# Two grouped-norm convolutions on one core: 32-wide products of both convolutions side by side, roots ahead of mid's normalization, x bands normalized on ScalarE

## The chip, the core and the metric

The kernel runs on one core of a Trainium2 chip. The metric is the device time of one launch in microseconds (us). Before the change the median of three runs is 901.29 us (901.25 to 901.67). Engines are called as the profile calls them: PE is TensorE (matmuls), PEld its weight loads, DVE is VectorE, ACT is ScalarE, POOL is GpSimd, SP is the engine that here only issues DMAs. Two independent runs of one kernel agree within about 0.2%.

## The reference

```python
def _gn(v, G=16, eps=1e-05):            # 32 channels, groups of 2
    g = v.reshape(B_, G, C_ // G, H_, W_)
    m = jnp.mean(g, axis=(2, 3, 4), keepdims=True)
    s = jnp.var(g, axis=(2, 3, 4), keepdims=True)
    return ((g - m) / jnp.sqrt(s + eps)).reshape(v.shape)
x = x + _L0_conv_ref(_gn(x), L0_conv_weight, L0_conv_threshold)   # 3x3, weights masked by a threshold
x = x + _L1_conv_ref(_gn(x), L1_conv_kernel, L1_conv_bias)        # 5x5, written with FFTs, plus bias
```

x is (16, 32, 128, 128) in float32. Both convolutions keep 32 channels and pad with zeros. The 5x5 one is written as a product of Fourier transforms, but is a plain 5x5 convolution of the padded image. The value between the two blocks is called mid.

## The kernel before

**Tiling.** An image is cut into two halves of 64 rows, so there are 32 halves (`HALVES`), half h being half h % 2 of image h // 2. A half lies in SBUF as four bands of 16 rows, one on each quarter of the 128 partitions (32 channels each), with 1 row of halo on each side for the 3x3 (`x_bands`, 6 slots, 128x2304 elements) and 2 rows for the 5x5 (`mid_bands`, 3 slots, 128x2560).

**Products in float16.** A float32 band is split into a float16 high part (`x3_hi`, `x5_hi`, written by ACT in `high3`, `high5`) and a float16 remainder (`x3_lo`, `x5_lo`, written by DVE in `low3`, `low5`); the weights likewise (`s3_hi`, `s3_lo`, `s5_hi`, `s5_lo`). Three products are summed in PSUM: high x high, high image x low weights, low image x high weights. There is one buffer of each of these four images, so the next one may be written only when PE has read the last one. The 3x3 sums lie in PSUM banks 0 to 3, the 5x5 sums in banks 4 to 7.

**pairs and singles.** A weight tile is 32 input channels (a quarter of the rows of the array) by either 64 columns (`pairs`, line 773: two neighbouring kernel rows at once, for two quarters of the output rows) or 32 columns (`singles`, line 791: the kernel row that is left over). Every matmul streams 512 columns. For one product of a half, the 3x3 takes 48 matmuls of each sort, the 5x5 160 pairs and 80 singles.

**The steps.** At step s PE does the 3x3 of half s and the 5x5 of half s - 3 (`LAG` = 3). Steps 0 to 2 are the lead (`lead_high`, `lead_low` and the small blocks between them, with only the 3x3), steps 3 to 31 run a loop body, `whole_step`, and steps 32 to 34 a second body, `last_steps`, with only the 5x5. Inside `whole_step` the order is high image 3x3, high image 5x5, low image 3x3, low image 5x5. A 3x3 result is taken out of PSUM by DVE (`take_conv3`, line 651, which adds x and makes mid); its drain (line 654) raises `bank3_go`, without which PE may not start the next step. A 5x5 result is taken by ACT (`take_conv5`, line 424) after `b5_whole`, POOL adds it to mid (line 360), SP stores it.

**Statistics.** DVE takes bn_stats of x (`stats_in`, line 560) and of mid (`stats_out`, line 659). Once per two steps the per-partition moments go through DRAM (`spread_stats`, `gather_stats`, issued by ACT) and come back to all partitions (`every_mv`). DVE then forms the group variance (`group_stats`, lines 592 to 600), ACT takes its square root (`take_root`, line 372) and DVE makes scale and bias from it (`scale_of`, lines 607 to 614). This is done in even steps s (where `exchanged(s - 1)` is not empty), for mid of the image just finished and for x of a coming image. `normalize3` scales a slot of x_bands in place (DVE, line 621), `normalize5` a slot of mid_bands (ACT, line 394).

**What sets the order.** Each engine runs its own program in the order in which it is written, and waits on semaphores; there is no planner. ACT's and DVE's order inside a step is that of the loops at lines 446 to 483 and 730 to 757. SP issues, in each step: the store of half s - 4, the load of x bands of half s + 6 (line 251, which waits on `norm1`), the moves of mid into mid_bands (16 DMAs from SBUF to SBUF, line 259), and x for half s + 2.

## Time and profile before

| | |
|---|---|
| median of three runs | 901.29 us |
| the profiled execution | 901.0 us |
| its span, first to last instruction | 899.2 us |
| mean granted clock of PE | 0.955 of full speed |
| PE busy / PEld busy | 794.9 us (88%) / 508.1 us (57%) |
| DVE busy | 611.0 us (68%) |
| ACT busy | 336.1 us (37%) |
| POOL busy | 234.5 us (26%) |
| bytes moved by DMA | 150.59 MB, mean 167 GB/s |
| chain that ended last | PE 75%, DVE 8%, issue 7%, ACT 4% |

Matmuls overlap one another in the array, so that the busy time of one (about 381 ns) says nothing of its cost; the distance from the start of one group of matmuls to the start of the next does. The chain that ended last follows the work back from the last instruction; a share of DVE and ACT in it is time in which PE was waiting for them.

### The profile page before, as it was taken

Reading aid. Unit: us, or ns where it says so; the run is one execution under the profiler, and the core shown is the slowest. Engines: PE = TensorE matmul, PEld = TensorE weight load, DVE = VectorE, ACT = ScalarE, POOL = GpSimd, SP = SyncE. Lnnn points to the kernel's source line nnn. Section 1 sums busy time; section 2 is a strip of 40 time slices with the busy share of each in tenths; the row PEclk is TensorE's granted clock in tenths of the full one; section 3 lists DMA queues with packets and bytes.
Section 4 is the critical chain, followed back from the end, with each engine's and each line's share of the span. In section 5 each row is a group of like instructions: output and inputs, shape, how many; then the busy total and the mean of one; then the engine's idle time right before and its main releaser. Section 6 shows DMA issues by size and latency. Waiting matters only on the chain.

```text
span 899.2 us, 67768 instructions
## 1 busy us (share of the span) xinstructions
PE 794.9 (88%) x32302; PEld 508.1 (57%) x32302; DVE 611.0 (68%) x949; ACT 336.1 (37%) x289; POOL 234.5 (26%) x165
## 2 busy tenths in 40 slices
PE   0785698989899898989899898989899898997895
PEld 0342365656567565756566575656566565664463
DVE  6676398786767697676767687686767585664141
ACT  0342234353524244353524244353524244352320
POOL 1014042322303232321303232321303232333031
PEclk9887999999999999999999999999999999999898
DMA  8989875978788686878888676978886554664313
GB/s 182 207 178 227 172 154 141 210 171 204 182 191 209 156 181 161 192 181 194 189 196 197 148 186 163 210 181 192 191 197 163 131 134 113 148 156 97 72 47 93
DMA packets 234118, 150.59 MB, mean 167 GB/s; under 512 B 18592, under 2 KB 227552, under 8 KB 229984
## 3 DMA queue, kind: packets, MB, share of 16 engines
q1 hardware_dynamic: 228768, 144.67, 70.3%
q10 hardware_dynamic: 4608, 4.23, 1.9%
q0 software_dynamic: 704, 1.25, 0.6%
q8 instruction: 16, 0.26, 0.1%
q14 instruction: 22, 0.18, 0.1%
HBM read 75.60 MB, written 33.59 MB: 121 GB/s over the span
## 4 chain that ended last, share of the span: by engine, by line
PE 75%; DVE 8%; issue 7%; ACT 4%; DVEq 2%; DMA 1%; POOL 1%; SPq 1%; ACTq 0%; POOLq 0%
PE psum L773 56%; PE psum L791 19%; ACT x_hi L379 3%; DVE mid L651 2%; DVEq L654 2%; DMA x_bands<-x_dram 1%; DVE bn_out L659 1%; DVE bn_in L560 1%; DVE x_lo L631 1%; ACT root L372 0%; SPq L251 0%; DVE x_lo L639 0%; DVE rinv L607 0%; DVE newton L609 0%; DVE newton L608 0%
## 5 line engine op out<-in xcount | busy, mean ns | idle before, releaser
L360 POOL TENSOR_TENSOR mid<-mid,conv_out 128x512 f32<-128x512 f32 x122 | 216.8, 1806 | 598.4 <-ACT conv_out L424 598.4
L773 PE MATMUL psum<-x_hi,s_hi 32*64 32x512 f16 x6656 | 211.8, 399 | 47.6 <-DVEq L654 37.8
L773 PE MATMUL psum<-x_hi,s_lo 32*64 32x512 f16 x6656 | 206.9, 391 | 1.9 <-issue 1.9
L773 PE MATMUL psum<-x_lo,s_hi 32*64 32x512 f16 x6656 | 200.7, 381 | 2.6 <-issue 2.6
L773 PEld LDWEIGHTS psum<-x_hi,s_hi 32*64 32x64 f16 x6656 | 107.1, 107 | 137.9 <-DVEq L654 44.6
L773 PEld LDWEIGHTS psum<-x_hi,s_lo 32*64 32x64 f16 x6656 | 126.9, 109 | 72.6 <-issue 16.0
L379 ACT ACTIVATE x_hi<-x_bands 128x2304 f16<-128x2304 f32 x32 | 68.0, 2126 | 265.4 <-PE psum L791 262.4
L651 DVE SCALAR_TENSOR_TENSOR mid<-psum,unscale,x_own 128x1024 f32<-128x1024 f32 x64 | 79.2, 1279 | 127.0 <-PE psum L791 126.5
L773 PEld LDWEIGHTS psum<-x_lo,s_hi 32*64 32x64 f16 x6656 | 111.7, 104 | 76.0 <-issue 13.9
L424 ACT ACTIVATE conv_out<-psum,bias,unscale 128x512 f32<-128x512 f32 x122 | 85.1, 777 | 61.4 <-PE psum L773 38.5
L639 DVE TENSOR_TENSOR x_lo<-mid_bands,x_hi 128x2560 f16<-128x2560 f32 x32 | 99.0, 3094 | 0.8 <-PE psum L773 0.5
L631 DVE TENSOR_TENSOR x_lo<-x_bands,x_hi 128x2304 f16<-128x2304 f32 x32 | 97.9, 3061 | 0.0
L791 PE MATMUL psum<-x_hi,s_hi 32*32 32x512 f16 x4096 | 76.1, 382 | 15.5 <-issue 9.0
L394 ACT ACTIVATE mid_bands<-mid_bands,nbias,gscale 128x2560 f32<-128x2560 f32 x32 | 80.8, 2524 | 22.1 <-DVE nbias L614 19.5
L387 ACT ACTIVATE x_hi<-mid_bands 128x2560 f16<-128x2560 f32 x32 | 74.8, 2339 | 36.8 <-PE psum L791 32.1
L659 DVE BATCH_NORM_STATS2 bn_out<-mid 128x6 f32<-128x512 f32 x128 | 79.1, 681 | 4.1
L791 PE MATMUL psum<-x_hi,s_lo 32*32 32x512 f16 x4096 | 78.1, 387 | 2.5 <-issue 2.5
L560 DVE BATCH_NORM_STATS2 bn_in<-x_bands 128x6 f32<-128x512 f32 x128 | 77.9, 668 | 1.3 <-DMA x_bands<-x_dram 1.1
L791 PEld LDWEIGHTS psum<-x_hi,s_hi 32*32 32x32 f16 x4096 | 52.5, 88 | 37.5 <-issue 24.8
L791 PE MATMUL psum<-x_lo,s_hi 32*32 32x512 f16 x4096 | 67.2, 381 | 2.0 <-issue 2.0
L791 PEld LDWEIGHTS psum<-x_hi,s_lo 32*32 32x32 f16 x4096 | 61.8, 88 | 5.2 <-issue 3.4
L791 PEld LDWEIGHTS psum<-x_lo,s_hi 32*32 32x32 f16 x4096 | 49.9, 88 | 23.3 <-issue 18.0
(77 smaller groups left out, 267.9 us busy)
## 6 DMA issues: line engine op xcount, KB each, us to landing
x_own<-x_dram SPq DMA_DIRECT2D x128, 256.0 KB, 5.0
mid_bands<-mid SPq DMA_DIRECT2D x372, 80.0 KB, 2.1
out_dram<-mid SPq DMA_DIRECT2D x116, 256.0 KB, 5.5
x_bands<-x_dram SPq DMA_DIRECT2D x96, 288.0 KB, 6.1
x_bands<-x_dram SPq DMA_DIRECT2D x32, 272.0 KB, 6.4
mid_bands<-mid SPq DMA_DIRECT2D x124, 64.0 KB, 2.0
every_mv<-mv_scratch ACTq DMA_DIRECT2D x16, 256.0 KB, 3.7
out_dram<-mid SPq DMA_DIRECT2D x24, 128.0 KB, 2.4
```

Of the source, the lines that this page charges most:

```text
L360: nc.gpsimd.tensor_tensor(m, m, conv_out[:, b, :], ALU.add).then_inc(out_added, 1)
L379: nc.scalar.activation(x3_hi[:, :, 2:2 + W], x_bands[:, h % XB_SLOTS, :, :], ACT.Copy).then_inc(hi3_done, 1)
L387: nc.scalar.activation(x5_hi[:, :, 2:2 + W], mid_bands[:, k % MB_SLOTS, :, :], ACT.Copy).then_inc(hi5_done, 1)
L394: nc.scalar.activation(v, v, ACT.Identity, bias=nbias[:, at], scale=gscale[:, at]).then_inc(act_scaled, 1)
L424: nc.scalar.activation(conv_out[:, b, :], psum[:, X5_BANK + b, :], ACT.Identity, bias=bias[:, 0:1], scale=unscale[:, 1:2]).then_inc(conv5_ ...
L560: nc.vector.bn_stats(bn_in[:, h // 2 % 2, h % 2, b, :], rows.rearrange("p a w -> p (a w)")).then_inc(bn_x, 1)
L631: nc.vector.tensor_tensor(x3_lo[:, :, 2:2 + W], x_bands[:, h % XB_SLOTS, :, :], x3_hi[:, :, 2:2 + W], ALU.subtract).then_inc(x3_lo_go, 1)
L639: nc.vector.tensor_tensor(x5_lo[:, :, 2:2 + W], mid_bands[:, k % MB_SLOTS, :, :], x5_hi[:, :, 2:2 + W], ALU.subtract).then_inc(x5_lo_go, 1)
L651: nc.vector.scalar_tensor_tensor(mid[:, h % MID_SLOTS, at, :], psum[:, X3_BANK + at.start:X3_BANK + at.stop, :], unscale[:, 0:1], x_own[:, ...
L659: nc.vector.bn_stats(bn_out[:, h % 2, b, :], mid[:, h % MID_SLOTS, b, :]).then_inc(bn_mid, 1)
L773: ins = nc.tensor.matmul(psum[2 * C * J:2 * C * (J + 1), bank + i, :].rearrange("p (a w) -> p a w", a=A), w[quad(i), at:at + 2, :].rearran ...
L791: ins = nc.tensor.matmul(psum[quad(j), bank + i, :].rearrange("p (a w) -> p a w", a=A), w[quad(i), at, :], src[quad(i), j + dy:j + dy + A ...
```

## The change

1. **PE.** Inside `whole_step` the order becomes: all pairs of the 3x3 (high and low image), the high-image pairs of the 5x5, all singles of the 3x3, all singles of the 5x5, and the low-image pairs of the 5x5. `last_steps` and the lead are ordered likewise. A new semaphore, `high3_whole`, tells when PE has read x3_hi for the last time; x5_hi is free after the 5x5's singles.
2. **ACT.** x bands are normalized on ACT (`normalize3` in the loop), after the 5x5 result is taken. Both square roots of an even step come before mid's normalization.
3. **DVE.** `normalize3` is left only for half 0. In an even step DVE forms both group variances, then both scales. `stats_in` of two halves is done in odd steps. `low3(s + 1)` stands at the end of step s and no longer in step s + 1. Its semaphore is split in two: one for SP (which frees the slot of x_bands) and one for PE behind a drain.
4. **Lead.** The scale of the 5x5 weights is formed before the second `take_conv3`, and PE's first block (`lead_start`) is placed in the program behind the lead's other blocks.

What PE's loop body is, before and after (x_hi with s_hi or s_lo is a high-image product, x_lo a low-image one; 64x512 is a pair, 32x512 a single). Before:

```order
L773 MATMUL psum<-x_hi,s_hi 64x512 x48
L773 MATMUL psum<-x_hi,s_lo 64x512 x48
L791 MATMUL psum<-x_hi,s_hi 32x512 x48
L791 MATMUL psum<-x_hi,s_lo 32x512 x48
L791 MATMUL psum<-x_hi,s_hi 32x512 x80
L791 MATMUL psum<-x_hi,s_lo 32x512 x80
L773 MATMUL psum<-x_hi,s_hi 64x512 x160
L773 MATMUL psum<-x_hi,s_lo 64x512 x160
L773 MATMUL psum<-x_lo,s_hi 64x512 x48
L791 MATMUL psum<-x_lo,s_hi 32x512 x128
L824 REGISTER_ALU
L773 MATMUL psum<-x_lo,s_hi 64x512 x160
```

After, the same body on the same engine:

```order
L777 MATMUL psum<-x_hi,s_hi 64x512 x48
L777 MATMUL psum<-x_hi,s_lo 64x512 x48
L777 MATMUL psum<-x_lo,s_hi 64x512 x48
L777 MATMUL psum<-x_hi,s_hi 64x512 x160
L777 MATMUL psum<-x_hi,s_lo 64x512 x160
L795 MATMUL psum<-x_hi,s_hi 32x512 x48
L795 MATMUL psum<-x_hi,s_lo 32x512 x48
L795 MATMUL psum<-x_lo,s_hi 32x512 x128
L795 MATMUL psum<-x_hi,s_hi 32x512 x80
L795 MATMUL psum<-x_hi,s_lo 32x512 x80
L834 REGISTER_ALU
L777 MATMUL psum<-x_lo,s_hi 64x512 x160
```

The counts are the same; the body goes from 64 to 32 columns or back four times before and twice after, the last block joining the next step's first.

What ACT does in an even step, from taking the 5x5 result on (line 372 is a root, line 394 a normalization, 379 and 387 the high parts of x and mid). Before:

```order
L424 ACTIVATE conv_out<-psum,bias,unscale 128x512 x4
L437 DMA every_mv<-mv_scratch 128x512
L372 ACTIVATE root<-gvar 128x1
L394 ACTIVATE mid_bands<-mid_bands,nbias,gscale 128x2560
L416 ACTIVATE mid_bands<-zeros 32x256
L379 ACTIVATE x_hi<-x_bands 128x18x128
L387 ACTIVATE x_hi<-mid_bands 128x20x128
L372 ACTIVATE root<-gvar 128x1
```

After, the same step:

```order
L424 ACTIVATE conv_out<-psum,bias,unscale 128x512 x4
L437 DMA every_mv<-mv_scratch 128x512
L394 ACTIVATE x_bands<-x_bands,nbias,gscale 128x2304
L404 ACTIVATE x_bands<-zeros 32x128
L372 ACTIVATE root<-gvar 128x1 x2
L394 ACTIVATE mid_bands<-mid_bands,nbias,gscale 128x2560
L416 ACTIVATE mid_bands<-zeros 32x256
L379 ACTIVATE x_hi<-x_bands 128x18x128
L387 ACTIVATE x_hi<-mid_bands 128x20x128
```

The second root has moved from behind both high parts to in front of mid's normalization, and the normalization of x bands is new on this engine.

What DVE does from the last variance of an even step to the start of the next step. Before:

```order
L600 SCALAR_TENSOR_TENSOR gvar<-sums 128x1
L560 BN_STATS bn_in<-x_bands 128x6 x4
L607 RECIPROCAL rinv<-root 128x1
L608 TENSOR_TENSOR newton<-gvar,rinv 128x1
L609 TENSOR_TENSOR newton<-newton,rinv 128x1
L610 TENSOR_SCALAR newton<-newton 128x1
L611 SCALAR_TENSOR_TENSOR gscale<-rinv,newton 128x1
L651 SCALAR_TENSOR_TENSOR mid<-psum,unscale,x_own 128x1024 x2
L659 BN_STATS bn_out<-mid 128x6 x4
L639 TENSOR_TENSOR x_lo<-mid_bands,x_hi 128x20x128
L631 TENSOR_TENSOR x_lo<-x_bands,x_hi 128x18x128
```

After, from the second scale of the same step on:

```order
L611 RECIPROCAL rinv<-root 128x1
L612 TENSOR_TENSOR newton<-gvar,rinv 128x1
L613 TENSOR_TENSOR newton<-newton,rinv 128x1
L614 TENSOR_SCALAR newton<-newton 128x1
L615 SCALAR_TENSOR_TENSOR gscale<-rinv,newton 128x1
L617 SCALAR_TENSOR_TENSOR nbias<-gmean,gscale 128x1
L656 SCALAR_TENSOR_TENSOR mid<-psum,unscale,x_own 128x1024 x2
L664 BN_STATS bn_out<-mid 128x6 x4
L635 TENSOR_TENSOR x_lo<-x_bands,x_hi 128x18x128
L644 TENSOR_TENSOR x_lo<-mid_bands,x_hi 128x20x128
```

The 3x3's low part (`x_lo<-x_bands`) now stands in front of the 5x5's, which begins the next step.

The diff, cut to its core:

```diff
@@ SP, in step s
                 if has3(s + XB_SLOTS):
-                    sp.wait_ge(norm1, s + 2)
+                    sp.wait_ge(low3_done, s + 1)
                     load_bands(s + XB_SLOTS)
@@ ACT: high3, high5
                 if h:
-                    act.wait_ge(c3_whole, h)
+                    act.wait_ge(high3_whole, h)
...
                 if k:
-                    act.wait_ge(b5_begun, k)
+                    act.wait_ge(a5_whole, k)
@@ ACT, in step s
+                if s == LAG:
                     take_root(gathered[0])
+                if s >= LAG and has3(s + 1):
+                    normalize3(s + 1)
+                if gathered and s > LAG:
+                    for stat in gathered:
+                        take_root(stat)
...
-                if len(gathered) > 1:
-                    take_root(gathered[1])
@@ DVE: low3
                 nc.vector.tensor_tensor(x3_lo[:, :, 2:2 + W], x_bands[:, h % XB_SLOTS, :, :], x3_hi[:, :, 2:2 + W],
-                                        ALU.subtract).then_inc(x3_lo_go, 1)
+                                        ALU.subtract).then_inc(low3_done, 1)
+                dve.drain().then_inc(x3_lo_go, 1)
@@ DVE, the lead
+            dve.wait_ge(w_loaded, 16 * 2 * Q)
+            largest(w5, 1)
+            power_of_two(1)
+            nc.vector.drain().then_inc(w5_bounded, 1)
             take_conv3(1)
-            stats_out(0)
             low3(2)
+            stats_out(0)
             stats_out(1)
             aggregate("mid", 0, mean_go)
-            dve.wait_ge(w_loaded, 16 * 2 * Q)
-            largest(w5, 1)
-            power_of_two(1)
-            nc.vector.drain().then_inc(w5_bounded, 1)
+            take_conv3(2)
             mean_of(("mid", 0))
-            take_conv3(2)
@@ DVE, in step s
                 low5(s - LAG)
-                if has3(s):
-                    low3(s)
                 if gathered:
                     dve.wait_ge(mv_in, 16 * exchange_number(s - 1))
-                    group_stats(gathered[0])
-                    scale_of(gathered[0])
-                if has3(s + 1):
-                    normalize3(s + 1)
+                for stat in gathered:
+                    group_stats(stat)
                 if len(gathered) > 1:
-                    group_stats(gathered[1])
-                if has3(s + 5):
-                    stats_in(s + 5, range(BANKS))
-                if len(gathered) > 1:
-                    scale_of(gathered[1])
+                    dve.wait_ge(norm1, s + 2)
+                for stat in gathered:
+                    scale_of(stat)
+                if s % 2:
+                    for h in (s + 3, s + 4):
+                        if has3(h):
+                            stats_in(h, range(BANKS))
                 if has3(s):
                     take_conv3(s)
                     stats_out(s)
...
+                if has3(s + 1):
+                    low3(s + 1)
@@ PE
+            def singles3():
+
+                singles(s3_hi, x3_hi, K3, X3_BANK)
+                singles(s3_lo, x3_hi, K3, X3_BANK).then_inc(high3_whole, 1)
                 singles(s3_hi, x3_lo, K3, X3_BANK).then_inc(c3_whole, 1)
...
+            def singles5():
 
                 pe.wait_ge(x5_lo_go, 1)
-                singles(s5_hi, x5_lo, K5, X5_BANK).then_inc(b5_begun, 1)
+                singles(s5_hi, x5_lo, K5, X5_BANK)
+                singles(s5_hi, x5_hi, K5, X5_BANK)
+                singles(s5_lo, x5_hi, K5, X5_BANK).then_inc(a5_whole, 1)
...
             with nc.body("whole_step", valid_engines=only):
                 hint = pe.mark_branch_hint_location()
-                high_image3()
-                high_image5()
-                low_image3()
-                low_image5(step)
+                pairs3_high()
+                pairs3_low()
+                pairs5_high()
+                singles3()
+                singles5()
+                pairs5_low(step)
```

## Rows read from the trace of the kernel before

**Rows 1.** Waits, longest first in total (us in total, times, longest).
```profile
DVE rinv L607 <- ACT root L372: 58.1, 32, 6.4
PE psum L773 <- DVEq L654: 37.8, 14, 2.8
```

**Rows 2.** Timeline (start us, us, engine, line), end of an even step, ACT, DVE, PE.
```profile
439.42 2.13 ACT L379 ACTIVATE x_hi<-x_bands 128x2304 f16<-128x2304 f32 x1 [2.29 <-PE psum L791]
...
441.71 2.34 ACT L387 ACTIVATE x_hi<-mid_bands 128x2560 f16<-128x2560 f32 x1 [0.17 <-issue]
443.95 0.19 ACT L372 ACTIVATE root<-gvar 128x1 f32<-128x1 f32 x1
444.17 0.17 DVE L607 RECIPROCAL rinv<-root 128x1 f32<-128x1 f32 x1 [4.07 <-ACT root L372]
...
445.14 2.48 DVE L651 SCALAR_TENSOR_TENSOR mid<-psum,unscale,x_own 128x1024 f32<-128x1024 f32 x2
...
447.72 1.89 PE L773 MATMUL psum<-x_hi,s_hi 32*64 32x512 f16 x48 [2.78 <-DVEq L654]
```

**Rows 3.** Windows: stretch, its us, busy us by engine, clock, DMA share, GB/s.
```profile
776.82:800.00 23.18, 23.18 (x1016) 15.46 (x1008) 17.80 (x25) 10.40 (x9) 8.91 (x4) 1.00 0.71 165
...
751.97:776.82 24.85, 24.85 (x1008) 16.35 (x1016) 14.92 (x15) 7.48 (x5) 3.11 (x3) 0.93 0.58 137
...
345.76:396.74 50.98, 48.20 (x2016) 32.66 (x2017) 37.59 (x57) 20.68 (x19) 13.65 (x9) 0.97 0.78 183
...
70.08:117.20 47.12, 30.07 (x1008) 16.76 (x1016) 26.18 (x45) 12.76 (x8) 8.43 (x16) 0.86 0.87 180
...
826.72:851.67 24.95, 22.11 (x720) 11.66 (x720) 3.14 (x14) 5.48 (x4) 4.43 (x4) 0.79 0.42 99
```

**Rows 4.** Timeline of PE, the matmul groups of a step at full clock.
```profile
421.55 1.51 PE L773 MATMUL psum<-x_hi,s_hi 32*64 32x512 f16 x48
422.87 1.53 PE L773 MATMUL psum<-x_hi,s_lo 32*64 32x512 f16 x48
424.32 0.93 PE L791 MATMUL psum<-x_hi,s_hi 32*32 32x512 f16 x48
...
425.66 1.40 PE L791 MATMUL psum<-x_hi,s_hi 32*32 32x512 f16 x80
426.75 1.40 PE L791 MATMUL psum<-x_hi,s_lo 32*32 32x512 f16 x80
428.08 4.61 PE L773 MATMUL psum<-x_hi,s_hi 32*64 32x512 f16 x160
432.50 4.60 PE L773 MATMUL psum<-x_hi,s_lo 32*64 32x512 f16 x160
```

**Rows 5.** Groups by line (count, busy us, mean ns of one, idle before).
```profile
L639 DVE TENSOR_TENSOR x_lo<-mid_bands,x_hi 128x2560 f16<-128x2560 f32 x32 | 99.0, 3094 | 0.8 <-PE psum L773 0.5
L631 DVE TENSOR_TENSOR x_lo<-x_bands,x_hi 128x2304 f16<-128x2304 f32 x32 | 97.9, 3061 | 0.0
L424 ACT ACTIVATE conv_out<-psum,bias,unscale 128x512 f32<-128x512 f32 x122 | 85.1, 777 | 61.4 <-PE psum L773 38.5 <-DVE mv L570 22.8
...
L659 DVE BATCH_NORM_STATS2 bn_out<-mid 128x6 f32<-128x512 f32 x128 | 79.1, 681 | 4.1
...
L621 DVE TENSOR_SCALAR x_bands<-x_bands,gmean,gscale 128x2304 f32<-128x2304 f32 x29 | 42.7, 1472 | 0.0
...
L394 ACT ACTIVATE x_bands<-x_bands,nbias,gscale 128x2304 f32<-128x2304 f32 x3 | 6.9, 2311 | 1.6 <-DVE nbias L614 1.2 <-issue 0.4
```

**Rows 6.** Timeline of DVE, the first group statistic of an even step.
```profile
428.72 0.88 DVE L592 SCALAR_TENSOR_TENSOR product<-every_mv,mix 128x128 f32<-128x128 f32 x1 [0.46 <-DMA every_mv<-mv_scratch]
```

**Rows 7.** Timeline of PE in the lead, steps 0 and 3.
```profile
35.82 2.77 PE L773 MATMUL psum<-x_lo,s_hi 32*64 32x512 f16 x42 [2.29 <-issue]
...
70.08 2.79 PE L773 MATMUL psum<-x_hi,s_hi 32*64 32x512 f16 x48 [1.78 <-POOL s_lo L348]
```

**Rows 8.** Timeline of SP's queue, the moves of mid in one step.
```profile
421.27 10.38 SPq L259 DMA_DIRECT2D mid_bands<-mid  x16
```

More of the change, by code:

```diff
@@ L144, in two_blocks @@
         a5_whole = sem("a5_whole")
-        b5_begun = sem("b5_begun")
+        high3_whole = sem("high3_whole")
         b5_whole = sem("b5_whole")
@@ L202, in two_blocks @@
         MOVES = Q * Q + 2
-        ON_SCALAR = range(1, LAG + 1)
         CLEARED = 4 + XB_SLOTS + 2 * MB_SLOTS
@@ L397, in normalize3 @@
             def normalize3(h):
-                act.wait_ge(scale_known, 1 if h < 2 else 2)
+                act.wait_ge(scale_known, ROOTS.index(("x", h // 2)) + 1)
                 act.wait_ge(x_bands_in[h % XB_SLOTS], 16 * Q * (h // XB_SLOTS + 1))
@@ L696, in _ @@
             scale_of(("x", 1))
-            take_conv3(1)
-            stats_out(0)
-            low3(2)
-            stats_out(1)
-            aggregate("mid", 0, mean_go)
             dve.wait_ge(w_loaded, 16 * 2 * Q)
@@ L705, in _ @@
             nc.vector.drain().then_inc(w5_bounded, 1)
+            take_conv3(1)
+            low3(2)
+            stats_out(0)
+            stats_out(1)
+            aggregate("mid", 0, mean_go)
+            take_conv3(2)
             mean_of(("mid", 0))
-            take_conv3(2)
             variance_of(("mid", 0))
@@ L720, in _ @@
             scale_of(("x", 2))
-            normalize3(LAG + 1)
+            take_conv3(LAG)
             stats_in(6, range(BANKS))
-            take_conv3(LAG)
+            stats_in(7, range(BANKS))
             stats_out(LAG)
-            stats_in(7, range(BANKS))
             aggregate("mid", LAG // 2)
             aggregate("x", (LAG + 3) // 2, mv_ready)
-            stats_in(8, range(BANKS))
+            low3(LAG + 1)
             for s in range(LAG + 1, STEPS):
@@ L802, in high_image3, with pairs3_low, pairs5_high, pairs5_low @@
                 pairs(s3_lo, x3_hi, K3, X3_BANK, every=bank3_go)
-                singles(s3_hi, x3_hi, K3, X3_BANK)
-                singles(s3_lo, x3_hi, K3, X3_BANK)
-            def low_image3():
+            def pairs3_low():
                 pe.wait_ge(x3_lo_go, 1)
                 pairs(s3_hi, x3_lo, K3, X3_BANK, every=x3_lo_go)
+            def singles3():
+                singles(s3_hi, x3_hi, K3, X3_BANK)
+                singles(s3_lo, x3_hi, K3, X3_BANK).then_inc(high3_whole, 1)
                 singles(s3_hi, x3_lo, K3, X3_BANK).then_inc(c3_whole, 1)
-            def high_image5():
+            def pairs5_high():
                 pe.wait_ge(x5_hi_go, 1)
-                singles(s5_hi, x5_hi, K5, X5_BANK, start=True)
-                singles(s5_lo, x5_hi, K5, X5_BANK)
-                pairs(s5_hi, x5_hi, K5, X5_BANK, every=x5_hi_go)
-                pairs(s5_lo, x5_hi, K5, X5_BANK).then_inc(a5_whole, 1)
-            def low_image5(step):
+                pairs(s5_hi, x5_hi, K5, X5_BANK, start=True, every=x5_hi_go)
+                pairs(s5_lo, x5_hi, K5, X5_BANK)
+            def singles5():
                 pe.wait_ge(x5_lo_go, 1)
-                singles(s5_hi, x5_lo, K5, X5_BANK).then_inc(b5_begun, 1)
+                singles(s5_hi, x5_lo, K5, X5_BANK)
+                singles(s5_hi, x5_hi, K5, X5_BANK)
+                singles(s5_lo, x5_hi, K5, X5_BANK).then_inc(a5_whole, 1)
+            def pairs5_low(step):
                 pe.reg_add(step, step, 1)
@@ L873, in _ @@
                 pe.br("lead_high")
+            with nc.body("lead_start", valid_engines=only):
+                mix_mean(("x", 0))
+                mix_variance(("x", 0))
+                keep_warm(16)
+                pe.wait_ge(w3_go, 1)
+                pe.br("lead_high")
             with nc.body("lead_mid", valid_engines=only):
@@ L892, in _ @@
             with nc.body("last_steps", valid_engines=only):
-                high_image5()
-                low_image5(step)
+                pairs5_high()
+                singles5()
+                pairs5_low(step)
                 pe.br_lt(step, STEPS, on_true="last_steps", on_false="all_done")
```

29 lines of the change are left out of this document (14 added, 15 removed).

## The prediction

> **What bounds the kernel now.** I read the chain of waits first: three quarters of it is PE, and what is not PE is DVE, ACT and "issue". The list of waits says where PE itself stands still: 14 times, for 37.8 us, for the drain behind take_conv3, and DVE before it for a square root of ACT [rows 1]. The timeline around one such place shows the chain. The 3x3 sums are whole when ACT can start x's high part at 439.42; ACT then writes both high parts and only afterwards takes the second root, at 443.95. DVE, idle for 4.07 us, makes the scale, takes the 3x3 result at 445.14, and PE starts the next step at 447.72 [rows 2]. The root's argument was ready long before; it stood behind work that waits for PE. So PE is held by an order of instructions, not by an engine that is full.
>
> Between these places PE runs without a gap: a step from 776.82 to 800.00 takes 23.18 us at full clock [rows 3]. A pair of steps takes 50.98 us [rows 3]: 2 x 23.18, a stall of 2.78 us plus 0.21 us in which the last matmuls would have overlapped the next ones (2.99), and a slow start. The step after a stall takes 24.85 us with a granted clock of 0.93, against 23.18 at 1.00: 1.67 us lost, as the clock falls from 2.4 to 1.2 GHz in the stall and PE's first pairs run at the lower level [rows 3]. There are 13 stalls in the loop, and by PE's timeline 11 of them are followed by a slow start. The sum closes: 28 steps (4 to 31) x 23.18 + 13 x 2.99 + 11 x 1.67 = 706.3 us, and these steps run from 117.20 to 823.17, 706.0 us.
>
> **PE's new order.** The matmuls are the same. 48 pairs take 1.32 us (421.55 to 422.87), but 1.45 where singles follow; 80 singles take 1.09 us (425.66 to 426.75), but 1.33 where pairs follow [rows 4]. A change of tile width so costs 0.13 and 0.24 us, 0.37 together. Before there are two of each in a step, after one of each: a step becomes 23.18 - 0.37 = 22.8 us. Bounds: nothing, if the cost belongs to the place and not to the change; 0.7 us, if the last change goes too.
> The Trainium skill (TensorEngine Tiling (Array Packing), Tiling Modes) says that changing the tiling mode drains the TensorE. Were that a full wait for one matmul's 0.38 us less its spacing, two changes fewer would give some 0.7 us per step, an estimate; by the rows it is half of that, and the rows decide.
>
> **The stall goes, if the new timetable holds.** I lay it out from the start of a step (0), with 27.6 ns per pair and 13.7 ns per single [rows 4]. PE: 3x3 pairs to 4.0; 5x5 pairs to 12.8; 3x3 singles, high3_whole at 14.3 and c3_whole at 15.0; 5x5 singles to 18.3; last pairs to 22.8. PE now leaves 7.8 us between the whole 3x3 and the next step; before it was some 5.4.
> ACT in an even step: 5x5 result 0.3 to 3.1 (4 x 0.78 with overlap [rows 5]), then the new normalization, 2.3 us plus 0.3 for the pad row, to 5.9. Both roots follow when the variances come. This normalization cost DVE 1.5 us and costs ACT 2.3 [rows 5]; ACT was busy for 20.7 of 50.98 us in a pair [rows 3] and gets to 26 of 45.6, so it lies beside PE's work. Behind the two roots are now queued mid's normalization, both high parts and the next 5x5 result.
> DVE in an even step: low5 to about 4.0; then the gathered moments. They landed 7.2 us into the step before (428.72 against 421.55 [rows 4, 6]), and are gathered 0.6 us earlier now. Two group statistics, 4.0 and 1.9 us, to 12.5; two scales of 1.2 to 15.0; take_conv3 15.2 to 17.8 with its drain; stats_out (4 x 0.68, overlapped, 2.5 us [rows 5]) to 20.3; low3(s + 1), 2.5 us when POOL is idle, 3.1 in the mean [rows 5], to about 23.0. It is wanted when PE has done its first 96 pairs, at 22.8 + 2.65 = 25.4: 2.4 us to spare. bank3_go at 17.8 is wanted at 22.8: 5 us to spare. In odd steps DVE has low5 and eight stats_in until 9, waits for c3_whole, and has two aggregations of 0.35 more before low3: 1.8 us to spare.
> ACT once more: mid's scale at 13.9, mid's normalization to 16.9, x's high part (2.1) to 19.1, mid's (2.3) to 21.5, and the 5x5 result at 23.1 on time. Its drain lets PE into the 5x5 pairs at 3.2 of the next step; PE wants it at 4.0: 0.8 us to spare, the thinnest of all.
> SP: 16 moves take 10.4 us to issue [rows 8], the other 12 to 16 DMAs of a step some 9 more at the same rate; 20 of 22.8 us, just enough. The load of x bands now waits for low3 instead of a normalization a step later, so it starts earlier; every other transfer is consumed a step or more after it is issued. DMA engines were busy for 0.78 of the time at 183 GB/s [rows 3]; the same bytes in 45.6 us are 205 GB/s at 0.87.
> So I take all 13 stalls and 11 slow starts as gone, with nothing in their place: 38.9 + 18.4, and 28 x 0.37 = 10.4. Together 67.7 us.
>
> **The lead.** In step 0 PE waited 2.29 us with nothing but issue before it in the middle of the low pairs, and the 42 pairs behind it took 2.7 instead of 1.2 us [rows 7]. It looks like code that had not arrived. The changed program places PE's first block behind the lead's others, so their code may be there by then: 2.3 + 1.5 us. Before step 3 PE waited 1.78 us for s5_lo of POOL [rows 7]; POOL now starts that work before take_conv3(1), which costs DVE 2.6 us there but frees the same 2.6 in front of mid's mean. About 6 us together. Bounds: 0 (the code is late as before, and the waits only change places) and 9 (all of it, and the clock holds better). Step 3, the first pass of the loop body, takes 47.1 us for 23 us of work [rows 3], with PE stopped every 128 matmuls: code again, with the same amount after; I leave it.
> **The tail.** Step 32 takes 24.95 us at a clock of 0.79 [rows 3], with a stop of 2.5 us after its first 139 matmuls. It now begins with pairs, which use up code half as fast, so most of this stop and part of the slow clock should go: 4 us. Bounds 0.4 (the changes of width alone) and 6.5.
>
> **Sum.** 899.2 + 1.8 around it = 901.0, less 67.7, 6 and 4, is 823.3. The medians lie 0.3 us above this execution: 824 us.
>
> **Rivals.**
> *The order of matmuls gives nothing.* The changes of width cost the same somewhere else, and lead and tail stay: 824 + 10 to 20, about 838. For it: 0.13 and 0.24 us are read at a few places only. Against: they are found at each change of a step and nowhere else. 0.12.
> *A shorter wait takes the stall's place.* ACT's drain for the 5x5 pairs has 0.8 us to spare. If mid's normalization slips by 2 us in even steps (moments that land later as the DMA engines are busier, or both group statistics at the 4.0 us of the one that ran beside POOL, where only one did before), PE waits some 1 us before its 5x5 pairs, 13 times, with a slow clock behind it of 1.7: 13 x 2.7 = 35, about 859 us. For it: DVE already waited 0.46 us for these moments [rows 6]. Against: three of the four margins are over 1.8 us. 0.13.
> The Trainium skill (SBUF — State Buffer, SBUF: two separate sides) has DVE and GpSimd share a port pair that one of them holds for a whole instruction, DVE's when it has two SBUF inputs. By that rule the second statistic would be slow too if POOL still adds at that time.
> *The stall stays.* The root is early, but DVE's longer even step makes take_conv3 late all the same, so only width, lead and tail gain: 901 - 20 = 881 us. It needs take_conv3 5 us after c3_whole. 0.03.
> *Slower than before.* low3 now stands at the very end of DVE's step, and PE wants it 2.65 us into the next one instead of 15. If it is late in every step, PE stops in the middle of its first pairs 28 times, each time with the clock's 1.7 us. The steps have 706.0 - 28 x 22.8 = 67.6 us to lose, 2.4 each; so it is slower from a wait of about 1.1 us, that is with DVE 3.5 us behind my timetable in even steps and 2.9 in odd ones. With a wait of 2.5 us: 824 + 28 x 4.2 = 941 us. For it: low3 took 3.6 us beside POOL. Against: at that time POOL is idle, and DVE has 45.6 us for about 33 us of work. 0.04.
>
> **Chances and range.** The forecast with its own bounds, 814 to 836, has 0.68. The range of 8 in 10, 812 to 848, adds the first rival and the lighter part of the second. A measurement of this kernel tells 0.2% (1.8 us) from no change. Faster 0.95; within 0.2% 0.01; slower 0.04.
>
> **What would show it.** Two equal steps of 22.8 us with a clock of 1.00; no wait of PE for take_conv3's drain; DVE waiting for PE before take_conv3 in both kinds of steps; the gaps before pairs and singles twice per step. Wrong would be: a regular gap before x_lo's or the 5x5's first pairs, steps of 23.2 us, or a first pass that moved by more than 6 us.

## The result, and the profile after

The changed kernel takes 835.83 us (median of 4 runs, 835.55 to 837.20); the kernel before took 901.48 us beside it (901.25 to 903.41). The ratio is 0.927, with a 95% interval of 0.9254 to 0.9287. The profiled execution took 835.55 us with a span of 833.7. The forecast was 824 us: the sign was right, and it was 12 us too low, so that the result lies at the very edge of the forecast's own bounds, 814 to 836. Single runs of the kernel before, taken with the experiments below, spread over 895.40 to 905.11 us, more than the 0.2% named at the start; so differences of 1 or 2 us are read from sets of runs whose ranges don't meet, or not at all.

The page of the kernel after, its first rows, the slices of PE's clock, and the chain:

```profile
span 833.7 us, 67844 instructions
...
PE 756.1 (91%) x32302; PEld 545.2 (65%) x32302; DVE 533.6 (64%) x907; ACT 407.9 (49%) x345; POOL 240.7 (29%) x165
...
PEclk9999969999999999999999999999999999999998
...
PE 88%; issue 4%; DVE 3%; DMA 1%; ACT 1%; SPq 1%; DVEq 0%; ACTq 0%; POOLq 0%; POOL 0%
```

PE is most of the chain now (88%), and its clock is at 90% or more of full in all slices but two. The span cut into its three parts, by the windows (stretch, its us, busy us of PE, weight load, DVE, ACT, POOL; clock, DMA share, GB/s): up to step 4, steps 4 to 31, and the rest:

```profile
0.00:120.79 120.79, 62.97 (x1918) 36.16 (x1926) 75.79 (x161) 33.62 (x24) 19.94 (x43) 0.92 0.96 195
120.79:759.53 638.74, 638.74 (x28235) 473.10 (x28223) 434.27 (x723) 356.43 (x304) 200.28 (x112) 1.00 0.85 190
759.53:833.70 74.17, 54.41 (x2168) 35.91 (x2160) 23.57 (x23) 17.88 (x17) 20.47 (x10) 0.94 0.31 76
```

In the 28 steps of the middle PE is busy for the whole stretch, 638.74 of 638.74 us, at a clock of 1.00. Before they took 705.97 us. So the three parts moved by -67.2 us (the steps), +3.6 (120.79 against 117.20) and -1.9 (74.17 against 76.03), together -65.5.

One step of PE after, which answers to [rows 4] and to the stall in [rows 2]:

```profile
394.51 1.51 PE L777 MATMUL psum<-x_hi,s_hi 32*64 32x512 f16 x48
...
398.49 4.59 PE L777 MATMUL psum<-x_hi,s_hi 32*64 32x512 f16 x160
...
407.42 0.93 PE L795 MATMUL psum<-x_hi,s_hi 32*32 32x512 f16 x48
...
411.59 1.38 PE L795 MATMUL psum<-x_hi,s_lo 32*32 32x512 f16 x80
412.90 4.61 PE L777 MATMUL psum<-x_lo,s_hi 32*64 32x512 f16 x160
417.31 1.52 PE L777 MATMUL psum<-x_hi,s_hi 32*64 32x512 f16 x48
```

No row has an idle time behind it, and none of those left out has, and the step takes 417.31 - 394.51 = 22.80 us. DVE and ACT in the same even step:

```profile
395.70 3.88 DVE L644 TENSOR_TENSOR x_lo<-mid_bands,x_hi 128x2560 f16<-128x2560 f32 x1 [0.56 <-issue]
402.14 1.26 DVE L596 SCALAR_TENSOR_TENSOR product<-every_mv,mix 128x128 f32<-128x128 f32 x1 [2.56 <-DMA every_mv<-mv_scratch]
...
409.85 2.48 DVE L656 SCALAR_TENSOR_TENSOR mid<-psum,unscale,x_own 128x1024 f32<-128x1024 f32 x2 [0.99 <-PE psum L795]
...
414.85 2.54 DVE L635 TENSOR_TENSOR x_lo<-x_bands,x_hi 128x2304 f16<-128x2304 f32 x1
```
```profile
404.87 0.20 ACT L372 ACTIVATE root<-gvar 128x1 f32<-128x1 f32 x1 [4.11 <-DVE gvar L604]
406.81 0.20 ACT L372 ACTIVATE root<-gvar 128x1 f32<-128x1 f32 x1 [1.74 <-DVE gvar L604]
407.86 2.53 ACT L394 ACTIVATE mid_bands<-mid_bands,nbias,gscale 128x2560 f32<-128x2560 f32 x1 [0.84 <-DVE nbias L617]
...
417.57 2.78 ACT L424 ACTIVATE conv_out<-psum,bias,unscale 128x512 f32<-128x512 f32 x4 [2.14 <-PE psum L777]
```

Both roots now come before mid's normalization. At 409.85 DVE waits for PE (0.99 us) and takes the 3x3 result while PE has 7.5 us of work left. low3 is done at 417.39, 0.08 us after the next step has begun; PE reads it behind its first 96 pairs, 2.6 us later.

What is left of waits is in the lead and the tail. PE's own rows in the list of waits (us in total, times, longest), which answer to [rows 1]:

```profile
PE psum L840 <- issue: 26.4, 1, 26.4
PE psum L795 <- issue: 14.7, 5, 6.3
PE psum L777 <- issue: 10.5, 5, 5.3
PE psum L777 <- ACTq L455: 6.1, 3, 2.9
...
PE psum L777 <- DVEq L659: 2.8, 2, 1.5
```

The 14 waits for take_conv3's drain, 37.8 us, have become two in the lead. The first row is new: before, PE's first matmul was at 19.89 us. Now it is at 26.41, with nothing but issue ahead of it. In the first pass of the loop body (step 3, 69.75 to 120.79; it answers to the fourth of [rows 3]) PE stands still time and again:

```profile
83.94 3.20 PE L777 MATMUL psum<-x_hi,s_hi 32*64 32x512 f16 x51 [5.32 <-issue]
...
92.37 2.62 PE L777 MATMUL psum<-x_hi,s_lo 32*64 32x512 f16 x83 [3.22 <-issue]
...
103.17 1.05 PE L795 MATMUL psum<-x_lo,s_hi 32*32 32x512 f16 x51 [4.18 <-issue]
...
112.42 0.61 PE L795 MATMUL psum<-x_hi,s_hi 32*32 32x512 f16 x3 [6.35 <-issue]
```

From one stop to the next lie 128 matmuls (51 + 77 from 83.94 on, for one), as before.

### The profile page after: what moved, and what is told of

It reads as the page before. It is cut to its first block, busy times and chain, and to the rows that moved or that the text cites. A ratio compares the mean times of both kernels' runs of the same rounds, so it can differ in the third digit from the quotient of the medians.

```text
span 833.7 us, 67844 instructions
## 1 busy us (share of the span) xinstructions
PE 756.1 (91%) x32302; PEld 545.2 (65%) x32302; DVE 533.6 (64%) x907; ACT 407.9 (49%) x345; POOL 240.7 (29%) x165
## 3 DMA queue, kind: packets, MB, share of 16 engines
q0 software_dynamic: 704, 1.25, 0.7%
## 4 chain that ended last, share of the span: by engine, by line
PE 88%; issue 4%; DVE 3%; DMA 1%; ACT 1%; SPq 1%; DVEq 0%; ACTq 0%; POOLq 0%; POOL 0%
PE psum L777 66%; PE psum L795 21%; DMA x_bands<-x_dram 1%; DVE x_lo L635 1%; DVE bn_out L664 1%; DVE mid L656 0%; DVEq L659 0%; SPq L251 0%; ACTq L455 0%; PE psum L852 0%; DVE bn_in L564 0%; ACT conv_out L424 0%; POOLq L57 0%; ACT x_hi L379 0%; SPq L275 0%
## 5 line engine op out<-in xcount | busy, mean ns | idle before, releaser
L360 POOL TENSOR_TENSOR mid<-mid,conv_out 128x512 f32<-128x512 f32 x122 | 220.8, 1844 | 538.7 <-ACT conv_out L424 538.7
L777 PE MATMUL psum<-x_hi,s_hi 32*64 32x512 f16 x6656 | 199.6, 381 | 15.7 <-ACTq L455 6.1
L777 PE MATMUL psum<-x_hi,s_lo 32*64 32x512 f16 x6656 | 197.6, 377 | 3.4 <-issue 3.4
L777 PEld LDWEIGHTS psum<-x_hi,s_hi 32*64 32x64 f16 x6656 | 128.2, 104 | 75.9 <-issue 10.3
L777 PEld LDWEIGHTS psum<-x_hi,s_lo 32*64 32x64 f16 x6656 | 143.1, 104 | 44.8 <-issue 4.8
L777 PEld LDWEIGHTS psum<-x_lo,s_hi 32*64 32x64 f16 x6656 | 106.5, 104 | 80.4 <-issue 11.9
L644 DVE TENSOR_TENSOR x_lo<-mid_bands,x_hi 128x2560 f16<-128x2560 f32 x32 | 92.8, 2901 | 18.4 <-PE psum L777 15.4
L635 DVE TENSOR_TENSOR x_lo<-x_bands,x_hi 128x2304 f16<-128x2304 f32 x32 | 81.1, 2535 | 0.2 <-issue 0.2
L394 ACT ACTIVATE x_bands<-x_bands,nbias,gscale 128x2304 f32<-128x2304 f32 x31 | 71.7, 2311 | 13.1 <-issue 10.7
L795 PEld LDWEIGHTS psum<-x_lo,s_hi 32*32 32x32 f16 x4096 | 57.6, 88 | 8.9 <-issue 7.6
```

Source lines behind the costliest of these rows:

```text
L360: nc.gpsimd.tensor_tensor(m, m, conv_out[:, b, :], ALU.add).then_inc(out_added, 1)
L394: nc.scalar.activation(v, v, ACT.Identity, bias=nbias[:, at], scale=gscale[:, at]).then_inc(act_scaled, 1)
L635: nc.vector.tensor_tensor(x3_lo[:, :, 2:2 + W], x_bands[:, h % XB_SLOTS, :, :], x3_hi[:, :, 2:2 + W], ALU.subtract).then_inc(low3_done, 1)
L644: nc.vector.tensor_tensor(x5_lo[:, :, 2:2 + W], mid_bands[:, k % MB_SLOTS, :, :], x5_hi[:, :, 2:2 + W], ALU.subtract).then_inc(x5_lo_go, 1)
L777: ins = nc.tensor.matmul(psum[2 * C * J:2 * C * (J + 1), bank + i, :].rearrange("p (a w) -> p a w", a=A), w[quad(i), at:at + 2, :].rearran ...
L795: ins = nc.tensor.matmul(psum[quad(j), bank + i, :].rearrange("p (a w) -> p a w", a=A), w[quad(i), at, :], src[quad(i), j + dy:j + dy + A ...
```

## Experiments

### The root alone, in the kernel before

```diff
@@ ACT of the kernel before, in step s
                     take_root(gathered[0])
+                if len(gathered) > 1:
+                    take_root(gathered[1])
...
-                if len(gathered) > 1:
-                    take_root(gathered[1])
```

> The kernel before with one edit: in an even step ACT takes both roots before it normalizes mid; all else (order of matmuls, DVE's normalization of x, low3 inside its own step) stays. My theory: the stall before odd steps is only the place of that root. DVE has the second variance 16 us into the even step, ends its statistics of x at 18.6, makes the scale at once and takes the 3x3 result at about 19.8 instead of 23.6; its drain comes at 22.4 where PE wants it at 23.2. So all 13 stalls (2.99 us) and 11 slow starts (1.67) go: 901.5 - 57 = 844 us. Rival (the new order of matmuls is what makes room, since before it the 3x3 sums are whole only 5.4 us before the next step): a stall of 1 us or more stays in each even step and most slow starts with it, 870 us or more.

Measured: 842.91 us (840.91 to 847.18) against 901.63; ratio 0.9367 (0.9329 to 0.9405). In the loop PE has no wait for take_conv3's drain left. The steps go from 325.93 to 349.11 and 372.27, 23.18 and 23.16 us, which is the old step at full clock. The second of these is an even step, and answers to [rows 2]; the root, the scale, the taking of the 3x3 result and PE's next step:

```profile
365.27 0.20 ACT L372 ACTIVATE root<-gvar 128x1 f32<-128x1 f32 x1 [4.78 <-DVE gvar L600]
367.53 0.14 DVE L607 RECIPROCAL rinv<-root 128x1 f32<-128x1 f32 x1
368.49 2.48 DVE L651 SCALAR_TENSOR_TENSOR mid<-psum,unscale,x_own 128x1024 f32<-128x1024 f32 x2
372.27 1.51 PE L773 MATMUL psum<-x_hi,s_hi 32*64 32x512 f16 x48
```

The root is ready 2.1 us before DVE, busy with its statistics of x, comes to it. DVE takes the 3x3 result at 368.49, and is done 1.3 us before PE begins the next step without a gap. So the place of one ACT instruction of 0.2 us is worth 58.7 us by the medians. In the profiled executions the 28 steps give 54.4 of it (705.97 against 651.6, 114.75 to 766.35), and lead and tail, which this edit does not touch, came out 2.5 and 1.9 us shorter. The stalls with their slow starts were 57.3 in the forecast; the first two steps of this loop are not yet at 23.18 (25.31 and 23.59), which is most of the difference.

### The second root put back, in the kernel after

```diff
@@ ACT, in step s
                 if gathered and s > LAG:
-                    for stat in gathered:
-                        take_root(stat)
+                    take_root(gathered[0])
...
                         high5(s + 1 - LAG)
+                if len(gathered) > 1:
+                    take_root(gathered[1])
```

> The changed kernel with the second root of an even step put back behind both high parts. My theory: DVE waits for it until 21 us into the step, takes the 3x3 result at 22.5, PE waits some 2.3 us at the start of 13 odd steps and again 1 to 2 us for low3, which now stands behind it, with a slow clock: 13 x 5 to 6.5 us, 900 to 920 us, no better than before the change. Rival (the new matmul order alone, with 7.8 us after the whole 3x3, absorbs a late root): under 850 us.

Measured: 909.64 us (906.76 to 910.53), ratio 1.0086 (1.0052 to 1.0120): the rest of the change with the old place of the root is 0.9% slower than the kernel before. PE's waits, and PE at one of the places:

```profile
PE psum L778 <- DVEq L638: 34.7, 15, 2.6
...
PE psum L778 <- DVEq L660: 24.9, 15, 1.7
```
```profile
301.58 1.54 PE L778 MATMUL psum<-x_hi,s_hi 32*64 32x512 f16 x48 [1.69 <-DVEq L660]
...
307.09 1.54 PE L778 MATMUL psum<-x_lo,s_hi 32*64 32x512 f16 x48 [2.64 <-DVEq L638]
```

In the timeline the first row waits for take_conv3, which stood behind the root. The second waits for low3, which stands behind take_conv3 on DVE, so one late root stops PE twice. This pair of steps takes 50.4 us (301.58 to 351.98) instead of 45.6, all of it at a clock of 1.00; the next pair takes 51.9 (to 403.86) at 0.97. In the new order the early root is what the rest rests on.

### low3 behind low5 in its own step

```diff
@@ DVE, in step s
                 if s > HALVES:
                     add_late(s - 1 - LAG)
+                if has3(s):
+                    low3(s)
...
-                if has3(s + 1):
-                    low3(s + 1)
```

> The changed kernel with low3 put back where it was, behind low5 in its own step. The new order of PE wants x's low image 2.65 us into the step; DVE would have it at about 7: a wait of 4.4 us in each of 28 steps, with a slow clock of 1 to 1.7 us behind it: 28 x 5.5 to 6 = 155 to 170 us more, some 995 us. It shows that the early low part is what the new order has to pay with. Rival (PE's wait is covered, since matmuls of the 5x5 are in its queue): under 850 us.

Measured, in one execution: 1009.08 us at a clock of 0.912, against 900.26. PE's wait, and PE in one step:

```profile
PE psum L776 <- DVEq L637: 111.3, 30, 4.3
```
```profile
322.23 1.52 PE L776 MATMUL psum<-x_hi,s_hi 32*64 32x512 f16 x48
...
329.02 2.79 PE L776 MATMUL psum<-x_lo,s_hi 32*64 32x512 f16 x48 [3.94 <-DVEq L637]
331.58 5.98 PE L776 MATMUL psum<-x_hi,s_hi 32*64 32x512 f16 x160
```

This is the slower rival made real. low3 is late in every step; here PE stops for 3.94 us, and the groups behind the stop run at the lower clock: 48 pairs in 2.79 us instead of 1.51, and 160 in 5.98 instead of 4.6. The step (322.23 to 351.80) is 29.57 us: 22.80, 3.94 of waiting and 2.8 for what runs slower. In the change as made, the move of low3 to the end of the step is needed for the new order of PE.

### Four changes of width instead of two

```diff
@@ PE, whole_step
                 pairs3_low()
-                pairs5_high()
                 singles3()
+                pairs5_high()
                 singles5()
```

> The changed kernel with the 3x3's singles moved in front of the 5x5's high pairs, so that the tile width changes four times in a step and not twice; nothing is wanted earlier than in the changed kernel. If a change of width costs 0.13 and 0.24 us wherever it stands: 28 x 0.37 = 10.4 us more, a step of 23.17 us, 846.2 us. If the cost belonged to other things of the old order: no change, 835.8 us. If the drain were a full matmul (0.35 us each), 28 x 0.7 = 20, 855 us.

Measured: 844.51 us (843.61 to 844.98), ratio 0.9372 (0.9347 to 0.9396), 8.7 us more than the change. From the start of step 4 (121.36) to that of step 31 (746.89) a step takes 23.17 us in the mean, 0.36 more than 22.81 in the change. The changed groups, of which one ends with a change and the other begins behind one:

```profile
332.51 1.53 PE L777 MATMUL psum<-x_lo,s_hi 32*64 32x512 f16 x48
333.97 0.93 PE L795 MATMUL psum<-x_hi,s_hi 32*32 32x512 f16 x48
...
335.30 0.94 PE L795 MATMUL psum<-x_lo,s_hi 32*32 32x512 f16 x48
336.17 4.61 PE L777 MATMUL psum<-x_hi,s_hi 32*64 32x512 f16 x160
```

48 pairs ahead of singles take 1.46 us, 1.32 otherwise; 48 singles ahead of pairs take 0.87, 0.67 otherwise. So two changes less are worth 28 x 0.36, about 10 us, against a forecast of 10.4. The profiled executions differ by 9.1 us, since the tail is 1.3 us shorter here (770.1 to 842.9) and the lead with its first pass 0.6 longer; no run says why. The same matmuls cost this by their order alone, and the first rival falls. The Trainium skill (TensorEngine Tiling (Array Packing), Tiling Modes) says that a change of tiling mode drains the TensorE. The sign agrees; a wait of a whole matmul at each change, 0.7 us for two, is not what the trace shows.

### The x bands normalized on DVE again

```diff
@@ ACT, in step s
-                if s >= LAG and has3(s + 1):
-                    normalize3(s + 1)
@@ DVE, in step s, behind low5
+                if has3(s + 1):
+                    normalize3_dve(s + 1)
                 if gathered:
                     dve.wait_ge(mv_in ...
```

> The changed kernel with x bands normalized on DVE again, between low5 and the wait for the gathered moments. My theory: DVE waited about 2.6 us there in even steps, so 1.6 us of work costs nothing, and in odd steps it has over 7 us before it takes the 3x3 result; no difference, 835.8 us within 0.2%. So moving it to ACT bought nothing by itself. Rival (DVE is short of time in even steps, ACT is not): low3 slips by 1.6 us and PE waits for it with a slow clock, 13 x 1 to 3 us more, 850 to 875 us.

Measured: 835.57 us (834.55 to 836.95), ratio 0.9276 (0.9251 to 0.9301): no difference from the change. Its steps take 22.8 us too. The operation fell into time in which DVE had been waiting for the gathered moments: that wait went from 66.0 us in total to 29.6.

### The lead: PE's first block, the loads, and mid's mean

Three kernels ask why PE starts at 26.41 instead of 19.89, and what that costs. The first puts PE's first block back in front:

```diff
@@ PE
             pe.wait_ge(mix_loaded, 16)
+            mix_mean(("x", 0))
+            mix_variance(("x", 0))
+            keep_warm(16)
+            pe.wait_ge(w3_go, 1)
...
-            pe.br("lead_start")
+            pe.br("lead_high")
```

> The changed kernel with PE's first block in front of the lead's other blocks again. In the changed kernel PE's first matmul started at 26.4 us instead of 19.9 with nothing but issue before it, while its input was ready at 19.7. My theory: that is the code of the block at the back arriving late; in front, the first matmul starts at 19.9, and a stop of some 2.3 us and slow pairs (1.5 us) come back in step 0. Net 6.5 - 3.8 = 2.7 us gained, if the first pass of the loop body is as long as before: 833 us. Rival (the late start has to do with the input's transfer, not with the place): no change.

Measured: 832.63 us (830.80 to 833.45), ratio 0.9254 (0.9238 to 0.9269), 3.2 below the change, with ranges that don't meet. PE's first row of it:

```profile
20.47 0.56 PE L840 MATMUL psum<-mv,mix 128*128 128x1 f32 x2 [20.47 <-DVE mv L574]
```

It waits for DVE now, not for itself. Step 3 starts at 65.91 and step 4 at 116.20.

The second leaves the block behind, and holds the loads that fill the DMA engines at the time:

```diff
@@ SP, the lead
+            sp.wait_ge(mean_go, 1)
             load_bands(2)
             load_bands(3)
             load_own(0)
```

> The changed kernel, but SP holds the loads of x bands 2 and 3 and of x until the first image's statistics are ready (about 19.7 us). If the code of PE's first block was late because 16 DMA engines were full of x, the first matmul starts at 19.9 instead of 26.4; the bands then come some 12 us later, and steps 1 to 3 pay for it: 835 to 850 us. If the code is late by itself (a far address), the first matmul stays at 26 us.

Measured: 834.24 us (832.64 to 834.81), ratio 0.9274 (0.9260 to 0.9289). PE's first row:

```profile
20.50 0.59 PE L841 MATMUL psum<-mv,mix 128*128 128x1 f32 x2 [20.50 <-DVE mv L575]
```

With the block in the same late place the first matmul comes 5.9 us earlier. From 10 to 20 us the DMA engines then carry 121 GB/s at a share of 0.57, where they carried 215 at 1.00 in the change and in the kernel before. So neither the place nor the loads alone make the block late: in front it comes in time beside full engines, and behind it comes in time beside half empty ones. That the bands come later has its price: the first matmul is level with the kernel that has the block in front, but step 3 starts at 68.92, 3.0 us behind it. It is less than the 835 to 850 us that had been expected, since the first pass then took 48.2 us and not 50.3.

The third takes the kernel with the block in front and forms mid's mean ahead of take_conv3(2), so that step 3 can start earlier:

```diff
@@ DVE, the lead
-            take_conv3(2)
             mean_of(("mid", 0))
+            take_conv3(2)
```

> The changed kernel with PE's first block in front and, before step 3, DVE's mean of mid in front of take_conv3(2) as in the kernel before. PE waited 2.8 us for that mean behind 2.5 us of take_conv3 in the changed kernel. Theory: 2.7 us from the first edit and 2.4 from the second, 831 us. Rival: the first pass of the loop body is held by the arrival of code (a stop at each 128 matmuls), and starting it 2.4 us earlier only makes its stops longer: 833 us.

Measured: 830.76 us (830.58 to 832.93), ratio 0.9243 (0.9228 to 0.9258); by their ranges this and the one with the block in front can't be told apart. Its trace tells more. Step 3 starts at 62.55, 3.4 us earlier, but step 4 at 115.34, only 0.9 earlier. The first pass took 52.8 us for 22.8 of work. What was gained ahead of it was given back: its stops with "issue" add up to 18.6 us against 16.1, and its waits for DVE and ACT to 3.2 against 0.3.

### Fewer loads beside the first pass

What sets the end of the first pass, if it is not its start? In the change DMA share is 1.11 and 222 GB/s between 60 and 110 us, against 1.03 and 210 before, and the last ten of these differ most:

```profile
100.00:110.00 10.00, 2.89 (x128) 1.83 (x128) 9.83 (x17) 6.09 (x5) 0.00 (x0) 0.71 1.03 224
100.00:110.00 10.00, 6.06 (x235) 3.78 (x233) 1.31 (x3) 0.00 (x0) 0.00 (x0) 1.00 0.71 164
```

The first row is the change, the second the kernel before. SP issued the loads of x bands 8 and 9 at much the same time in both (95.93 to 100.3, and 93.58 to 100.7). The moves of mid of half 3 came 11.5 us earlier, at 101.30 instead of 112.79, because in PE's new order the 3x3 is whole sooner in the body.

The next kernel is the last one, with the loads of x bands 8 and 9 put behind these moves (they go at 113.05 instead of 92.30):

```diff
@@ SP, the lead, and in step s
             load_own(4)
-            load_bands(8)
...
-                if has3(s + XB_SLOTS):
+                if has3(s + XB_SLOTS) and s > LAG:
                     sp.wait_ge(low3_done, s + 1)
                     load_bands(s + XB_SLOTS)
...
+                    if s == LAG:
+                        sp.wait_ge(low3_done, s + 1)
+                        load_bands(8)
+                        load_bands(9)
```

> The version with PE's first block in front and mid's mean early (830.8 us), and the loads of x bands 8 and 9 issued behind the moves of mid of half 3 instead of at the beginning of the loop's first pass; they are not needed before step 5. In that pass (62.6 to 115 us) PE stops at each 128 matmuls, and the DMA engines are over 100% busy from 60 to 110 us. If the stops are code that waits behind data on these engines, 2.3 MB less in the way (some 10 us at 220 GB/s) shortens them: first pass of 47 us or less instead of 52.8, 826 us. Rival (the code comes at its own pace of 6 to 9 us per 128 matmuls): 830.8 us.

Measured: 823.69 us (822.71 to 825.11), ratio 0.9154 (0.9126 to 0.9182). It is the best version, 12.1 us below the change. Its first pass, in windows and in PE's stops:

```profile
80.00:90.00 10.00, 4.21 (x80) 1.90 (x83) 0.00 (x0) 0.00 (x0) 0.00 (x0) 0.71 1.12 211
90.00:100.00 10.00, 6.36 (x303) 4.17 (x301) 8.21 (x22) 5.76 (x6) 0.00 (x0) 0.84 0.73 130
100.00:110.00 10.00, 9.12 (x359) 6.23 (x335) 8.92 (x11) 6.25 (x5) 1.04 (x1) 0.94 0.46 105
```
```profile
85.79 4.90 PE L780 MATMUL psum<-x_hi,s_lo 32*64 32x512 f16 x83 [6.08 <-issue]
...
97.40 1.47 PE L798 MATMUL psum<-x_lo,s_hi 32*32 32x512 f16 x51 [3.35 <-issue]
...
101.15 0.44 PE L798 MATMUL psum<-x_hi,s_hi 32*32 32x512 f16 x3 [0.47 <-issue]
...
104.55 3.50 PE L780 MATMUL psum<-x_lo,s_hi 32*64 32x512 f16 x115 [0.41 <-issue]
```

Up to 97 us the stops are as long as in the kernel that this one is built on (6.08 against 5.80, 3.35 against 3.62); the loads that were moved would have begun at 92. Behind that they shrink: the stop of 6.35 us in the change (5.49 in the kernel with mid's mean moved) is 0.47. A part of this is PE's own slowness, for it does the 128 singles ahead of this stop at a clock of 0.57. The distance from border to border leaves that out: it is 3.75 us (97.40 to 101.15), where it was 8.96 (96.91 to 105.87). Step 4 starts at 107.68, after a first pass of 44.7 us instead of 52.8. So the long stops belong to what the DMA engines carry at the time.

A floor is left. In step 32 of the change, behind the loop, PE runs through new code once more:

```profile
780.21 0.84 PE L795 MATMUL psum<-x_hi,s_lo 32*32 32x512 f16 x37 [1.44 <-issue]
```
```profile
778.77:780.21 1.44, 0.00 (x1) 0.00 (x0) 0.00 (x0) 0.00 (x0) 0.00 (x0) 1.00 0.00 0
```

This stop falls where the DMA engines carry nothing at all. From the border before it (776.75, behind a stop of 1.58 us) it is 3.46 us, near the 3.75 above, and 128 singles at full clock take 1.76. So new code has a pace of its own, 3.4 to 4.1 us for 128 matmuls where the engines carry little (101.15 to 104.55 in the last kernel, 780.21 to 784.35 here): pairs (3.5 us) nearly hide it, singles don't. The rival of a pace of 6 to 9 us is wrong in size, not in kind.

## Why the prediction was right in the loop and wrong at the ends

**The stall, right.** The forecast gave 38.9 us for 13 stalls and 18.4 for the slow starts, from the place of the second root. With the root alone moved the kernel gained 58.7 us, 54.4 of it in the steps, and with the root alone moved back the whole gain and more was gone.

**The changes of width, right.** 22.81 us is the mean of the 28 steps, and 22.8 was forecast. Undone by itself, the step was 23.17 again, so a pair of changes costs 0.36 us where 0.37 was forecast. Both terms together were 67.7 us, and the steps gave 67.2.

**The timetable, right in its end, not in all its parts.** The moments landed 7.6 us into the step. I had laid them out at 6.6, 0.6 earlier than the 7.2 of before. DVE waited 2.56 us for them. That did not move the end, since the two statistics took 2.7 and 1.95 us and not 4.0 and 1.9: POOL's additions ended 1.05 us into the first. low3 ended 22.9 us into the step, where 23.0 was forecast, and ACT started the 5x5 result 0.3 us into the next one, as forecast. So the rival of the shorter wait did not come about. The case of DVE's normalization says more: that operation lay in a wait of DVE and cost nothing on either engine, so its move was no part of the gain. I had costed it at nothing on ACT and had not asked what it was worth on DVE.

**The slower rival, its price too low.** I gave each wait of PE for low3 a slow clock of 1.7 us behind it. Where the wait was made real, a stop of 3.94 us was followed by 2.8 us; behind the stops of 1.69 and 2.64 us of the kernel with the root put back there was none in the pair shown. Its limit, a wait of 1.1 us, does not follow from the 2.4 us a step named beside it, which less 1.7 leaves 0.7; it needs the 77 us of the whole kernel, lead and tail with it.

**The lead, wrong: the step "their code may be there by then".** I forecast -6 with bounds 0 and 9 on the side of a gain, and it came to +3.6, outside them. Two parts of it failed. PE's first block, placed behind the others, did not bring their code earlier for nothing: it came itself 6.5 us later, beside loads of x that fill the DMA engines from 10 us on. The stop of 2.29 us in [rows 7] did go, and by step 3 the lead had made the loss good (69.75 against 70.08). The wait of 1.78 us for the 5x5's low weights went too, but PE then waited 1.59 and 2.82 us for mid's moments and mean, 0.23 and 1.25 before; so that term of the 6 us gave nothing. With the block in front, step 3 started at 65.91, 4.2 us ahead of before. How much of this is the edit's is open: the kernel with only the root moved has the lead of before, and came to step 3 at 67.48, with a better clock of PE in the lead (the 42 pairs behind the same stop took 1.4 us there and not 2.7).

Then the second part: "code again, with the same amount after; I leave it". The first pass of the loop body took 51.0 us and not 47.1, and with the block in front 50.3; three kernels whose step 3 started at 69.75, 65.91 and 62.55 started step 4 at 120.79, 116.20 and 115.34. Its length was not the work's but, as the last kernel shows, that of the code's way beside busy DMA engines. The change had made these busier: the moves of mid of half 3 now run behind the loads of x bands 8 and 9 without a pause. That the loads may go earlier, which I had written down, has little part in it; in this pass they lost one wait of 3.0 us. Which of the two made the pass longer was not tested by itself. That the amount of code is the same says nothing of its time. The 3.9 us are no chance: the first pass took 47.1 and 47.3 us in the two kernels with the old order of PE, and 50.7 to 51.8 in the change and in the three experiments with PE's first block behind, low3 early and the loads not held.

**The tail, mis-sized.** Forecast -4, measured -1.9. In step 32 the clock was 0.93 instead of 0.79, and the step took 23.86 us (762.68 to 786.54) instead of 24.95, but its stops did not go: they were 2.53 and 0.28 us, and are 0.18, 1.58, 1.44 and 0.54. They have moved to where the code then runs out, the singles above all, and one of 1.44 us stands where the DMA engines are idle. That is 0.9 more of stops where I had taken most of 2.5 away; pairs do use up code half as fast, but the singles behind them come upon the same borders.

The sum, in the same terms: -67.2, +3.6 and -1.9 against -67.7, -6 and -4. Of the 12 us by which the forecast was low, 9.6 are the lead's.

## What to carry to other kernels

Look in the list of waits for an engine that waits for something small (a root, a scale) that was ready to run long before: the order of one 0.2 us instruction on an engine that was busy for 37% of the time was worth 58.7 us here. Where the busy engine itself is never idle, count how often its kind of instruction changes; the order alone may hold a percent. And where stops with "issue" ahead of them come at a fixed count of instructions in a first pass, treat the instructions as one more transfer: read the DMA share beside them, and move loads that are not yet needed away from there, before touching the work. Where the share is low and stops are left, only slower use of the code (here pairs before singles) would hide them; no run here tests that.

## What was not expected of the hardware

PE stood still every 128 matmuls in the first pass of the change, for 1.1 to 6.4 us each, at a DMA share of 1.06 over the pass. The profile has DMA queues of the kind "instruction" (packets, MB, share of 16 engines), and one of them fits. In the first pass of the change, 69.75 to 120.79:

```profile
q8 instruction: 7, 0.11, 1.1%
```

That is a packet of about 16 KB for each of the seven borders that PE crosses there. In the 28 steps behind it, in which PE never stops, this queue moved nothing, and in lead and tail it moved packets again. So code that is run for the first time comes through the same DMA engines as the data, in pieces of 128 matmuls with their weight loads. That q8 is PE's queue is read from this count and not named by the profile.

In the last kernel the late stops were 0.4 to 0.5 us at 105 to 130 GB/s; in step 32 of the change one of 1.44 us stood at 0 GB/s. The first matmul of the program came at 26.41 or at 20.5 us with the same code, depending on whether the loads from x bands 2 on ran beside it.

The low part of mid took DVE 3.88 us where POOL's additions had begun 0.08 us before it (395.62), and 2.83 where it began 0.79 us before them (417.64 and 418.43); there POOL's first addition took 3.18 us, where 1.84 is its mean. The Trainium skill (SBUF — State Buffer, SBUF: two separate sides) has the engine that starts first hold the shared ports for its whole instruction. The two rows agree with that; that it is the ports was not tested by itself.
